# Self-attention's maxima from four column tiles, next to the value steps

## The chip, the core and the metric

The kernel runs on one core of a Trainium2 chip. Its engines work from queues of their own and wait for one another by semaphores: TensorE (PE; its weight loads are PEld), VectorE (DVE), ScalarE (ACT), GpSimd (POOL), and SyncE (SP), which here only issues transfers. The metric is the device time of one execution in microseconds. TensorE's results go to eight banks of on-chip memory, each 128 partitions by 512 floats.

## The reference

A decoder layer on x of 4 batches x 1024 tokens x 256 features, in float32. With 16 heads of 16 features:

```
qkv = layernorm(x) @ w_qkv                       # self-attention in chunks of 128 tokens
scores = q_chunk @ [k_previous_chunk, k_chunk].T / 4
scores masked where key > query, and where the previous chunk does not exist
x = x + softmax(scores) @ [v_previous, v_chunk] @ w_out
x = x + cross_attention(layernorm(x), ctx 77 keys, key mask)
x = x + ffn(layernorm(x))                        # 8-bit fake-quantised, inner width 704
```

So each query of self-attention sees the 128 keys of the chunk before its own and the keys of its own chunk up to itself.

## The kernel before, in words

Attention is cut into 16 jobs: self-attention (s) and cross-attention (x) of each batch, each in two halves a and b of eight heads, in the order S0a S0b S1a S1b S2a X0a S2b X0b S3a X1a S3b X1b X2a X2b X3a X3b. Each job has two groups, 0 and 1, of four heads. A group passes three kinds of TensorE steps. (Below, S1b-0 is group 0 of job S1b.)

A **maximum step** (lines 656 to 672) takes one chunk c of 128 queries. For each of the four heads one matmul forms scores of 128 queries against 256 keys (queries stationary, keys moving; the operands are bfloat16 parts whose products add up to float32 accuracy, 96 rows), two heads to a bank. One more matmul a bank adds the causal mask to the own-chunk columns of both heads. VectorE then reduces 4 x 256 columns to four negated maxima a query (line 1179). After the eighth chunk, "rows" splits the maxima into three bfloat16 parts with four short VectorE operations, "turnm" transposes them on TensorE (line 687), ScalarE copies them out (962) and issues a transfer (964) that puts them as three more rows below the queries. A **score step** (699) then multiplies with keys stationary, 99 rows: its result is already less the maximum, ScalarE takes the exponential (974), GpSimd clears what the causal mask hides (1451). A **value step** (737) multiplies with the values, 17 columns wide, on four column tiles: tile_position (0, 32i) puts each head on a quarter of the array's columns, and the four run at once. Cross-attention has its own three forms (677/679, 706/709, 748).

Results rotate over six banks. A maximum or score step needs two neighbouring ones, so three of them fit; a projection (qk 630, v 640, out 759) takes one. A step waits until the reader of its banks is through.

The order of all steps is written once, for all engines, by attention_order(). The table PLACE gives spans of each kind of work as shares of a period (LENGTH: 24.5 for a group of self-attention, 9.6 for cross); steps are spread evenly over their span and sorted by time. During the period of a group the maxima of the *next* group are placed ("max s0s" and so on). BEHIND says how many steps later a follower comes: turnm three after rows, a value step two score steps behind. Every engine goes through this list in order; one that waits holds up all that is behind it.

## Time and profile before

| | us |
|---|---|
| median of 3 runs | 851.69 (844.95 to 858.25) |
| profiled execution, span from first to last instruction | 849.0 |
| PE busy | 684.6 (81%) |
| DVE busy | 545.8 (64%) |
| ACT busy | 415.1 (49%) |
| POOL busy | 188.8 (22%) |
| self-attention maxima on DVE (line 1179), 128 reductions | 145.1 |
| mean granted TensorE clock | 0.911 |

Profile times count from the first instruction. The profiled execution's own time is its span of 849.0, 2.7 below the median. The granted clock of a stretch is 1.00 where TensorE had its full 2.4 GHz and 0.50 where it had 1.2 GHz. In a timeline row, the time is the start of the first of "xN" instructions and the length reaches to the end of the last; consecutive matmuls overlap, so the cost of a step is read from its start to the start of the next.

### The profile page before, as it was taken

The page shows a single profiled execution, that of the slowest core. Times are in us where ns is not written, and L with a number is a line of the kernel's source. Part 1 is how long each engine was busy: PE and PEld are TensorE (multiplying, and loading weights), DVE is VectorE, ACT ScalarE, POOL GpSimd, SP SyncE. Part 2 cuts the span into 40 slices and gives each one's busy share as a digit, 9 for nine tenths or more (in the row PEclk, how much of TensorE's full clock was granted, in tenths as well). Part 3 has the DMA queues.
Part 4 walks back from the last instruction along what each step waited for, and adds up shares of the span by engine and source line. Part 5 has one row for each costly group of instructions (what it writes and reads, how often), then busy time and mean ns, then how long its engine had stood idle before and what let it go on. Part 6 is the DMA issues. An engine that isn't in the chain of part 4 may idle for free.

```text
span 849.0 us, 14814 instructions
## 1 busy us (share of the span) xinstructions
PE 684.6 (81%) x5391; PEld 414.9 (49%) x5396; DVE 545.8 (64%) x975; ACT 415.1 (49%) x610; POOL 188.8 (22%) x231
## 2 busy tenths in 40 slices
PE   2579999989996998999979989897886784488565
PEld 1346565655653564556644644464543442233254
DVE  6277658866864456677636874556745651679996
ACT  2324665536463444555334446433343352399775
POOL 5002131312231120310113123002002000044436
PEclk9988999999997997999988989997998786699989
DMA  7534243502622153243222432331237112000013
GB/s 215 125 106 143 54 128 81 149 3 90 165 77 61 21 170 105 46 141 78 86 50 96 109 96 69 97 95 42 70 85 211 23 42 53 0 1 2 0 65 135
DMA packets 59557, 71.83 MB, mean 85 GB/s; under 512 B 25003, under 2 KB 36447, under 8 KB 59487
## 3 DMA queue, kind: packets, MB, share of 16 engines
q1 hardware_dynamic: 53391, 68.01, 29.2%
q10 hardware_dynamic: 6096, 2.88, 1.3%
q8 instruction: 44, 0.72, 0.4%
q14 instruction: 26, 0.21, 0.1%
HBM read 17.74 MB, written 4.72 MB: 26 GB/s over the span
## 4 chain that ended last, share of the span: by engine, by line
PE 49%; DVE 22%; issue 8%; ACT 7%; SPq 6%; DMA 6%; ACTq 1%; POOL 1%; POOLq 0%; DVEq 0%
PE banks L630 8%; PE banks L759 7%; PE banks L667 5%; PE banks L737 5%; DVE mneg L1179 4%; PE banks L699 4%; PE banks L640 3%; PE banks L748 3%; SPq L523 3%; PE banks L670 3%; DVE xn L1143 2%; SPq L517 2%; PE banks L706 2%; PE banks L709 2%; DVE tops L1358 2%
## 5 line engine op out<-in xcount | busy, mean ns | idle before, releaser
L1179 DVE TENSOR_REDUCE mneg<-banks 128x4 f32<-128x1024 f32 (+1 forms) x128 | 145.1, 1151 | 68.0 <-PE banks L670 67.5
L974 ACT ACTIVATE big<-banks 128x1024 f32<-128x1024 f32 (+1 forms) x128 | 123.0, 974 | 105.4 <-PE banks L699 101.7
L1451 POOL TENSOR_SCALAR_AFFINE_SELECT big<-big 128x512 f32<-128x512 f32 x128 | 83.1, 650 | 391.6 <-ACT big L974 390.9
L978 ACT ACTIVATE big<-banks 77x1024 f32<-77x1024 f32 x64 | 65.3, 1020 | 86.3 <-PE banks L709 81.8
L667 PE MATMUL banks<-big 96*128 96x256 bf16 (+1 forms) x512 | 94.5, 280 | 13.4 <-DMA big<-parts 9.8
L630 PE MATMUL banks<-xnT,weights 128*128 128x512 f32 x192 | 92.9, 617 | 3.9 <-ACT big L978 3.9
L699 PE MATMUL banks<-big 99*128 99x256 bf16 (+1 forms) x512 | 79.3, 280 | 13.3 <-DMA big<-m3t 5.7
L1183 DVE TENSOR_REDUCE mneg<-banks 128x8 f32<-128x616 f32 x64 | 50.3, 793 | 57.7 <-PE banks L679 57.6
L737 PE MATMUL banks<-big 128*17 128x256 f32 (+1 forms) x1152 | 79.0, 366 | 1.0 <-POOL big L1451 0.6
L670 PE MATMUL banks<-causal,identb 128*128 128x256 bf16 x256 | 72.9, 288 | 0.0
L667 PEld LDWEIGHTS banks<-big 96*128 96x128 bf16 x512 | 47.9, 103 | 45.9 <-issue 26.6
L699 PEld LDWEIGHTS banks<-big 99*128 99x128 bf16 x512 | 45.0, 101 | 48.3 <-issue 32.5
L803 PE MATMUL banks<-oe,weights 128*128 128x512 bf16 x187 | 46.8, 394 | 11.0 <-DVE big L1352 4.4
L630 PEld LDWEIGHTS banks<-xnT,weights 128*128 128x128 f32 x192 | 35.7, 197 | 38.1 <-issue 31.4
L677 PE MATMUL banks<-big 96*128 96x77 bf16 x512 | 43.1, 214 | 13.2 <-DMA big<-kparts 9.6
L706 PE MATMUL banks<-big 99*77 99x256 bf16 x256 | 51.1, 282 | 3.1 <-DVE big L1169 1.1
L677 PEld LDWEIGHTS banks<-big 96*128 96x128 bf16 x512 | 35.3, 108 | 32.9 <-issue 19.8
L709 PE MATMUL banks<-maskt,identb 77*77 77x512 bf16 x128 | 50.4, 394 | 0.0
L987 ACT COPY oe<-banks 128x512 f32<-128x512 f32 x64 | 37.2, 585 | 26.8 <-DMA oTx<-oe 10.9
L1224 DVE TENSOR_TENSOR xs<-banks,xs 128x512 f32<-128x512 f32 x32 | 22.1, 689 | 37.6 <-PE banks L759 37.6
L618 PE MATMUL banks<-ident,xn 128*128 128x128 f32 x128 | 23.7, 319 | 23.9 <-DVE xn L1143 23.5
L748 PE MATMUL banks<-big 77*17 77x256 f32 x512 | 42.7, 426 | 0.0
(155 smaller groups left out, 1163.8 us busy)
## 6 DMA issues: line engine op xcount, KB each, us to landing
big<-parts SPq DMA_DIRECT2D x282, 128.0 KB, 2.5
oc<-sums SPq DMA_DIRECT2D x16, 512.0 KB, 4.6
oTs<-oe SPq DMA_DIRECT2D x64, 64.0 KB, 2.3
out_dram<-oTs SPq DMA_DIRECT2D x16, 256.0 KB, 2.1
xs<-in_x_dram SPq DMA_DIRECT2D x3, 1024.0 KB, 5.8
big<-oe SPq DMA_DIRECT2D x32, 64.0 KB, 2.3
oTx<-oe SPq DMA_DIRECT2D x32, 64.0 KB, 2.3
big<-kparts SPq DMA_DIRECT2D x96, 9.6 KB, 1.8
```

The costliest lines, as they stand in the source:

```text
L630: t = e.matmul(bank(p), w[:, i, :], xnT[T][:, i, blk * 512:blk * 512 + 512], start=(i == 0), stop=(i == 1))
L667: e.matmul(bank(p, j)[:, i * 256 + lo * 128:i * 256 + 256], Q[0:96, hh, c * 128:c * 128 + 128], K[0:96, hh, (c - 1 + lo) * 128:(c + 1) * 1 ...
L670: t = e.matmul(bank(p, j).rearrange("p (s n) -> p s n", s=2)[:, :, 128:256], identb[:, :], causal[:, :].rearrange("p (a n) -> p a n", a=1) ...
L677: e.matmul(bank(p, j)[:, i * KX:i * KX + KX], Q[0:96, i, (c + j) * 128:(c + j) * 128 + 128], xks[r][0:96, i, :], start=(i == 0), stop=Fals ...
L699: t = e.matmul(bank(p, i // 2)[:, (i % 2) * 256:(i % 2) * 256 + n], ks[r][0:99, i, j * 128:j * 128 + 128], qs[r][0:99, i, j * 128:j * 128 ...
L706: e.matmul(bank(p, z)[0:KX, i * 256:i * 256 + 256], xks[r][0:99, 2 * z + i, :], qs[r][0:99, 2 * z + i, j * 256:j * 256 + 256], start=(i == ...
L709: t = e.matmul(bank(p, z)[0:KX, :].rearrange("p (i n) -> p i n", i=2), identb[0:KX, 0:KX], keep.to_broadcast([KX, 2, 256]), start=False, s ...
L737: t = e.matmul(acc[:, col // 512][32 * i:32 * i + 17, col % 512:col % 512 + z - a], va[f][:, j, 4 * g + i, :], P[:, i, a:z], start=new, st ...
L748: t = e.matmul(acc[:, j // 2][32 * i:32 * i + 17, (j % 2) * 256:(j % 2) * 256 + 256], xv[r][0:KX, i, 0:17], pt[u][0:KX, i * 256:i * 256 + ...
L974: e.activation(pt[u].rearrange("p (i n) -> p i n", i=4)[:, :, 0:n], pair(p).rearrange("p j (s n) -> p (j s) n", s=2)[:, :, 0:n], ACT.Exp, ...
L1179: e.tensor_reduce(M.rearrange("p (h c) -> p h c", h=4)[:, :, c], pair(p).rearrange("p j (s n) -> p (j s) n", s=2)[:, :, lo * 128:256], AX. ...
L1451: e.affine_select(out=P[:, :, 0:128], in_=P[:, :, 0:128], compare_op=ALU.is_ge, fill=0.0, base=0, pattern=[[0, 4], [1, 128]], channel_mult ...
```

## The change

**Queries in another order.** The qk projection of the queries reads its tokens permuted: for each half of 512 tokens, Q now holds a (which 32 of a chunk, 0 to 3), then the chunk t (0 to 3), then the 32 tokens. 128 neighbouring columns of Q are thus 32 queries of each of four chunks.

**Maximum step.** Step c = 4G + a takes these 128 queries. For each head there are four matmuls of 32 queries, one on each column tile, each over the keys of the chunk before (128) and the first 32a + 32 keys of its own: 160, 192, 224 or 256 columns. Chunk 0 has none before it, so there a matmul over key 0 repeated 128 times and one over the own keys stand in. The mask is added to the last 32 columns alone, by four matmuls of 2 x 32 columns a bank. A step has 24 matmuls (28 in the first half) where it had 6. The reduction reads 4 x (160 + 32a) elements a partition.

**Score step.** It gathers its queries from the new order; step 3 needs two matmuls of 128 a head instead of one of 256.

**Order.** beside() moves each maximum step of self-attention to the time of the nearest value step, directly behind it; rows stays where it was unless a step comes later.

```diff
@@ -123,6 +123,12 @@
     return [(span[0] + (span[1] - span[0]) * i / len(steps), step) for i, step in enumerate(steps)]
 
 
+def beside(timed, at):
+
+    near = [min(at, key=lambda v: abs(v - t)) for t, _ in timed]
+    return [(v + 0.0005, step) for v, (_, step) in zip(near, timed)]
+
+
 def stats_steps(kind, b):
     return [("stats", kind, b, c) for c in range(NC)] + [("root", kind, b, 0, NC)]
 
@@ -192,7 +198,8 @@
         job, units = JOBS[n], UNITS[JOBS[n][0]]
         kind, length = job[0], LENGTH[job[0]]
         nxt = JOBS[n + 1] if n + 1 < len(JOBS) else None
-        put([(-0.001, ("force", "rows"))] + over(PLACE["tail " + kind], tail))
+        ends = over(PLACE["tail " + kind], tail)
+        put([(-0.001, ("force", "rows"))] + ends)
         scores = over(PLACE["score " + kind], [("score", job, g, j) for j in range(units)])
         for j in range(units):
             put([scores[j]])
@@ -200,7 +207,12 @@
                 put([(scores[j][0] + 0.002, ("val", job, g, j - BEHIND["val"], False))])
         tail = [("val", job, g, j, j == units - 1) for j in range(units - BEHIND["val"], units)]
         if p + 1 < 2 * len(JOBS):
-            put(over(PLACE[f"max {kind}{g}{nxt[0] if g else kind}"], max_steps(p + 1)))
+            tops = over(PLACE[f"max {kind}{g}{nxt[0] if g else kind}"], max_steps(p + 1))
+            if JOBS[(p + 1) // 2][0] == "s":
+                values = [t for t, _ in ends] + [scores[j][0] + 0.002 for j in range(BEHIND["val"], units)]
+                tops = beside(tops[:-1], values) + tops[-1:]
+                tops[-1] = (max(tops[-1][0], tops[-2][0]), tops[-1][1])
+            put(tops)
         last = JOBS[n - 1] if n else ("s", 0, 0)
         if g == 0:
             if nxt:
@@ -627,8 +639,10 @@
                     e.wait_ge(a_xnT, 2 * n_of["turned", kind, b, 4 * blk])
                     w = wq_of(job, z)
                     for i in range(2):
-                        t = e.matmul(bank(p), w[:, i, :], xnT[T][:, i, blk * 512:blk * 512 + 512],
-                                     start=(i == 0), stop=(i == 1))
+                        tokens = xnT[T][:, i, blk * 512:blk * 512 + 512]
+                        if kind == "s" and z == 0:
+                            tokens = tokens.rearrange("p (t a b) -> p a t b", t=4, a=4)
+                        t = e.matmul(bank(p), w[:, i, :], tokens, start=(i == 0), stop=(i == 1))
                     t.then_inc(t_qk, 1)
                 elif k == "v":
                     _, job, c0 = s
@@ -660,16 +674,28 @@
                         if n_of[s] == 1:
                             e.wait_ge(p_set, 4)
                             e.wait_ge(d_set, 1)
-                        lo = 1 if c == 0 else 0
+                        G, a = divmod(c, 4)
+                        own = 32 * a + 32
                         for j in range(2):
                             for i in range(2):
                                 hh = 2 * j + i
-                                e.matmul(bank(p, j)[:, i * 256 + lo * 128:i * 256 + 256], Q[0:96, hh, c * 128:c * 128 + 128],
-                                         K[0:96, hh, (c - 1 + lo) * 128:(c + 1) * 128], start=(i == 0), stop=False,
-                                         skip_group_check=True)
-                            t = e.matmul(bank(p, j).rearrange("p (s n) -> p s n", s=2)[:, :, 128:256], identb[:, :],
-                                         causal[:, :].rearrange("p (a n) -> p a n", a=1).to_broadcast([128, 2, 128]),
-                                         start=False, stop=True, skip_group_check=True)
+                                for u in range(4):
+                                    q = Q[0:96, hh, c * 128 + 32 * u:c * 128 + 32 * u + 32]
+                                    to = bank(p, j)[32 * u:32 * u + 32, i * 256:i * 256 + 128 + own]
+                                    k0 = (4 * G + u) * 128
+                                    if k0:
+                                        e.matmul(to, q, K[0:96, hh, k0 - 128:k0 + own], start=(i == 0), stop=False,
+                                                 tile_position=(0, 32 * u), skip_group_check=True)
+                                    else:
+                                        e.matmul(to[:, 0:128], q, K[0:96, hh, 0:1].to_broadcast([96, 128]), start=(i == 0),
+                                                 stop=False, tile_position=(0, 0), skip_group_check=True)
+                                        e.matmul(to[:, 128:128 + own], q, K[0:96, hh, 0:own], start=False, stop=False,
+                                                 tile_position=(0, 0), skip_group_check=True)
+                            for u in range(4):
+                                late = causal[:, 32 * u:32 * u + 32].rearrange("p (s n) -> p s n", s=1)
+                                t = e.matmul(bank(p, j)[32 * u:32 * u + 32, :].rearrange("p (s n) -> p s n", s=2)[
+                                    :, :, 96 + own:128 + own], identb[:, 32 * u:32 * u + 32], late.to_broadcast([128, 2, 32]),
+                                    start=False, stop=True, tile_position=(0, 32 * u), skip_group_check=True)
                     else:
                         e.wait_ge(d_mask, 2)
                         for j in range(2):
@@ -694,11 +720,20 @@
                         if AT[job] < 2:
                             e.wait_ge(p_ones, r + 1)
                     if job[0] == "s":
-                        n = 256 if j < 7 else 128
                         for i in range(4):
-                            t = e.matmul(bank(p, i // 2)[:, (i % 2) * 256:(i % 2) * 256 + n],
-                                         ks[r][0:99, i, j * 128:j * 128 + 128], qs[r][0:99, i, j * 128:j * 128 + n],
-                                         start=(i % 2 == 0), stop=True, skip_group_check=True)
+                            to = bank(p, i // 2)[:, (i % 2) * 256:(i % 2) * 256 + 256]
+                            k = ks[r][0:99, i, j * 128:j * 128 + 128]
+                            q = qs[r][0:99, i, :].rearrange("p (g a u b) -> p g u a b", g=2, a=4, u=4)
+                            G, u = divmod(j, 4)
+                            if u < 3:
+                                t = e.matmul(to, k, q[:, G, u:u + 2, :, :], start=(i % 2 == 0), stop=True,
+                                             skip_group_check=True)
+                            else:
+                                t = e.matmul(to[:, 0:128], k, q[:, G, 3, :, :], start=(i % 2 == 0), stop=True,
+                                             skip_group_check=True)
+                                if G == 0:
+                                    t = e.matmul(to[:, 128:256], k, q[:, 1, 0, :, :], start=False, stop=True,
+                                                 skip_group_check=True)
                     else:
                         keep = maskt[0:KX, j * 256:j * 256 + 256].rearrange("p (a n) -> p a n", a=1)
                         for z in range(2):
@@ -1175,10 +1210,9 @@
                     M = mneg[:, rows_n[job, g] % 2, :]
                     e.wait_ge(t_max, n_of[s])
                     if job[0] == "s":
-                        lo = 1 if c == 0 else 0
                         e.tensor_reduce(M.rearrange("p (h c) -> p h c", h=4)[:, :, c],
-                                        pair(p).rearrange("p j (s n) -> p (j s) n", s=2)[:, :, lo * 128:256], AX.X, ALU.max,
-                                        negate=True).then_inc(d_max, 1)
+                                        pair(p).rearrange("p j (s n) -> p (j s) n", s=2)[:, :, 0:160 + 32 * (c % 4)],
+                                        AX.X, ALU.max, negate=True).then_inc(d_max, 1)
                     else:
                         e.tensor_reduce(M.rearrange("p (h c) -> p c h", h=4)[:, c:c + 2, :],
                                         pair(p)[:, :, 0:4 * KX].rearrange("p j (s n) -> p j s n", s=4), AX.X, ALU.max,
```

On TensorE, the end of S0a-0, from its turnm (before L687, now L713) to the first score step of S0a-1 (L699, now L729; with 128 columns it is the group's last). Before (L667 and L670 are maximum steps, L737 value steps, L618 transposes of normalised x):

```order
L687 MATMUL banks<-identb,m 96x128
L699 MATMUL banks<-big 128x256 x4
L737 MATMUL banks<-big 17x256 x4
L667 MATMUL banks<-big 128x256 x2
L670 MATMUL banks<-causal,identb 128x2x128
L618 MATMUL banks<-ident,xn 128x128 x8
L699 MATMUL banks<-big 128x128 x4
L737 MATMUL banks<-big 17x256 x4
```

Rows that only repeat the maximum steps are left out here: two whole ones stand before the L618 row, two more after the last row, then the first score step of S0a-1. Now (L772 value, L732 the last score step, L630 the transposes):

```order
L713 MATMUL banks<-identb,m 96x128
L772 MATMUL banks<-big 17x256 x4
L732 MATMUL banks<-big 128x128 x4
L772 MATMUL banks<-big 17x256 x4
L729 MATMUL banks<-big 128x256 x4
L630 MATMUL banks<-ident,xn 128x128 x8
L772 MATMUL banks<-big 17x256 x4
L690 MATMUL banks<-big 32x128
L692 MATMUL banks<-big 32x32
L687 MATMUL banks<-big 32x160 x3
```

Between turnm and the next group's first score step stood a score step more, the transposes and four maximum steps; now there are two value steps and the last score step. The next group's maxima begin after that first score step, seven in a row.

On VectorE, the same place (before L1179, now L1213, is the reduction of a maximum step; L1193 to L1199, now L1227 to L1233, are rows; L1143, now L1178, normalises x; L1152, now L1187, belongs to a projection). Before:

```order
L1199 TENSOR_TENSOR m<-mr,m 128x32
L1179 TENSOR_REDUCE mneg<-banks 128x4
L1143 TENSOR_SCALAR xn<-xs,mv,rstd 128x256 x4
L1179 TENSOR_REDUCE mneg<-banks 128x4 x7
L1152 TENSOR_TENSOR big<-banks,parts 128x512
```

Now:

```order
L1233 TENSOR_TENSOR m<-mr,m 128x32
L1178 TENSOR_SCALAR xn<-xs,mv,rstd 128x256 x4
L1213 TENSOR_REDUCE mneg<-banks 128x4 x8
L1187 TENSOR_TENSOR big<-banks,parts 128x512
```

The eight reductions were spread over score and value steps of two groups; now they all belong to the start of the second.

On VectorE again, X0a, whose two groups carry the maxima of X0a-1 (L1183, now L1217) and of S2b-0 (L1179, now L1213); L1154, now L1189, belongs to a projection. Before:

```order
L1183 TENSOR_REDUCE mneg<-banks 128x2x4 x2
L1179 TENSOR_REDUCE mneg<-banks 128x4
L1183 TENSOR_REDUCE mneg<-banks 128x2x4 x2
L1179 TENSOR_REDUCE mneg<-banks 128x4
L1193 CAST m<-mneg 128x32
...
L1179 TENSOR_REDUCE mneg<-banks 128x4
L1206 RECIPROCAL ls<-ls 128x64
L1179 TENSOR_REDUCE mneg<-banks 128x4 x4
L1154 SCALAR_TENSOR_TENSOR big<-banks,bias,parts 128x512
```

Now:

```order
L1217 TENSOR_REDUCE mneg<-banks 128x2x4 x4
L1227 CAST m<-mneg 128x32
...
L1240 RECIPROCAL ls<-ls 128x64
L1213 TENSOR_REDUCE mneg<-banks 128x4 x8
L1189 SCALAR_TENSOR_TENSOR big<-banks,bias,parts 128x512
```

On TensorE the eight maximum steps now stand between the two groups' score steps: six, a value step, two. The same happens in X0b and X1a. TensorE's runs of column-tiled work (value steps, and now maximum steps) number 168 in both orders.

## Rows read from the trace of the kernel before

**Rows 1.** The page: tenths of the time an engine is busy, 40 slices.
```profile
PE   2579999989996998999979989897886784488565
DVE  6277658866864456677636874556745651679996
PEclk9988999999997997999988989997998786699989
```
**Rows 2.** Busy time and granted clock, a stretch of S0b to S1b.
```profile
core 0: us, PE busy (x) PEld busy (x) DVE busy (x) ACT busy (x) POOL busy (x), PEclk, DMA share, GB/s
150.00:250.00 100.00, 92.44 (x825) 58.53 (x818) 71.04 (x125) 53.16 (x78) 25.47 (x37) 0.98 0.36 96
```
**Rows 3.** TensorE's timeline, value step 0 and maximum steps 4, 5 in S1b-0.
```profile
218.12 0.62 PE L737 MATMUL banks<-big 128*17 128x256 f32 x8
218.67 0.39 PE L667 MATMUL banks<-big 96*128 96x256 bf16 x2
...
219.44 0.38 PE L667 MATMUL banks<-big 96*128 96x256 bf16 x2
...
220.10 0.60 PE L699 MATMUL banks<-big 99*128 99x256 bf16 x4
```
**Rows 4.** TensorE's timeline, a first maximum step (151.12), and two value steps together.
```profile
151.12 0.28 PE L667 MATMUL banks<-big 96*128 96x128 bf16 x2
...
151.58 0.38 PE L699 MATMUL banks<-big 99*128 99x256 bf16 x2
...
152.78 0.84 PE L737 MATMUL banks<-big 128*17 128x256 f32 x16
153.55 0.61 PE L699 MATMUL banks<-big 99*128 99x256 bf16 x4
```
**Rows 5.** Groups by shape: the reductions, with busy us and mean ns.
```profile
L1179 DVE TENSOR_REDUCE mneg<-banks 128x4 f32<-128x1024 f32 x112 | 134.1, 1218 | 41.9 <-PE banks L670 41.5
L1179 DVE TENSOR_REDUCE mneg<-banks 128x4 f32<-128x512 f32 x16 | 11.0, 686 | 26.0 <-PE banks L670 26.0
```
**Rows 6.** TensorE's timeline: start of the very first maxima, and the projection after five.
```profile
42.44 0.37 PE L667 MATMUL banks<-big 96*128 96x128 bf16 x2 [8.79 <-DMA big<-parts]
...
48.37 0.86 PE L630 MATMUL banks<-xnT,weights 128*128 128x512 f32 x1
```
**Rows 7.** SP's timeline: first of its issues for X0a.
```profile
245.16 9.66 SPq L523 DMA_DIRECT2D big<-parts  x12
```
**Rows 8.** TensorE's timeline: the first maximum step of X0a, in S2a.
```profile
267.30 0.40 PE L677 MATMUL banks<-big 96*128 96x77 bf16 x4 [4.72 <-DMA big<-kparts]
```
**Rows 9.** TensorE's timeline in X0a: turnm, and the first score step of S2b-0.
```profile
324.79 0.26 PE L687 MATMUL banks<-identb,m 128*96 128x128 bf16 x1
...
329.47 0.37 PE L699 MATMUL banks<-big 99*128 99x256 bf16 x1 [2.43 <-DMA big<-m3t]
```
**Rows 10.** Windows: score step 5 to the work behind the last maximum; S0a, S0b, S1a, S1b.
```profile
79.12:93.94 14.82, 13.05 (x137) 8.51 (x134) 12.61 (x20) 7.39 (x12) 3.85 (x6) 1.00 0.02 3
124.55:135.92 11.37, 10.93 (x124) 7.00 (x120) 9.28 (x13) 5.78 (x10) 3.17 (x5) 1.00 0.22 53
164.99:185.23 20.24, 16.44 (x145) 10.99 (x142) 14.91 (x22) 7.38 (x12) 3.85 (x6) 0.92 0.14 33
221.19:236.47 15.28, 13.25 (x137) 8.46 (x134) 12.59 (x21) 7.39 (x12) 3.94 (x6) 1.00 0.38 85
```
**Rows 11.** TensorE's timeline in S1a-1: the output projection of batch 0.
```profile
179.13 3.39 PE L759 MATMUL banks<-weights,oTs 128*128 128x256 f32 x8 [1.99 <-DVE oTs L1216]
```
**Rows 12.** Windows: the wait of rows 9, what follows it, and a feed-forward stretch.
```profile
326.40:329.40 3.00, 0.64 (x10) 0.38 (x6) 2.93 (x8) 1.02 (x1) 0.00 (x0) 0.90 0.36 109
329.40:339.00 9.60, 9.53 (x55) 4.91 (x56) 5.32 (x10) 3.98 (x5) 1.27 (x2) 0.50 0.41 133
816.00:824.00 8.00, 5.91 (x48) 4.40 (x48) 8.00 (x9) 6.70 (x7) 5.17 (x5) 1.00 0.36 127
```
**Rows 13.** Window: the densest 24 matmuls in a row.
```profile
148.10:149.14 1.04, 1.03 (x24) 0.83 (x25) 0.28 (x1) 1.01 (x2) 0.64 (x1) 1.00 0.38 120
```

## The prediction

> **What bounds the kernel now.** I read the page's slices first. TensorE stands at nines from the third slice to about the 28th, VectorE mostly at six to eight: in self-attention the kernel runs at TensorE's pace [rows 1]. A window says the same: in 100 us TensorE is busy for 92.44, VectorE for 71.04 [rows 2]. Then I read the timeline step by step, each from its start to the start of the next. A maximum step (four matmuls of 256 columns, two masks of 256) takes 219.44 to 220.10, 0.66 us, back to back with its neighbours [rows 3]. That is 0.11 for 256 columns, or 0.43 ns a column. A value step takes 218.12 to 218.67, 0.55 [rows 3], but two together, the second of half the columns, take 152.78 to 153.55, 0.77 [rows 4]: part of a lone step is the change into and out of column tiling, which a neighbour shares. So what TensorE saves comes off the time only where it runs back to back. Last I looked for places where it stands, and for who holds it.
>
> **The change, part by part**
>
> *The step on TensorE.* Four tiles run at once in a value step. If the new matmuls do too, a round of four costs the columns of one: 160, 192, 224 or 256 at 0.43 ns, 0.07 to 0.11. Four rounds and two short mask rounds (64 columns, 0.03 each) make 0.33, 0.39, 0.44 and 0.50 for a = 0 to 3. Eight steps cost 3.3, against 0.46 (151.12 to 151.58) for the first [rows 4] and seven of 0.66: 5.1. That saves 1.8 a group, 28 in sixteen groups, gross. No row shows bfloat16 rounds of this length. The bounds are this, and a round as long as one of 256 columns now, six times 0.11: 0.66, no saving. I take the short one, because the value step is the same arrangement; the other end is a rival.
>
> *The reduction on VectorE.* 1024 elements take 1.218, 512 take 0.686 [rows 5], about 1.04 ns an element. So 640, 768, 896 and 1024 take 0.82, 0.95, 1.09 and 1.22: 8.2 for eight, where it was 9.2. VectorE's 145.1 falls to about 130. That counts where TensorE waits for VectorE. The mean, 1.02, is over twice TensorE's new 0.42, and this matters next.
>
> *Order.* Three pairs of banks fit. A run of more than three maximum steps therefore goes at VectorE's pace of 1.02. What the new order saves in changes of tiling is nothing: 168 column-tiled runs before and after. What it costs has to be added place by place.
>
> 1. S0a-0. Five steps take 42.44 to 48.37, 5.93, at half clock [rows 6]. Twice the new prices for five steps are 4.0, and three steps behind them also get cheaper: 2.4 gained.
> 2. Maxima that are needed in group 1 of S0a, S0b, S1a, S1b, S2b, S3b stand in ones and twos next to value steps of group 0; TensorE has no long wait there. 1.8 less about 0.35 of waits for a bank: 1.4 each, 8.6. In the last two, three steps are at half clock and gain about 0.7 more each. S0a has five in a row, 0.8 lost. Together 9.2 gained.
> 3. S2a and S3a: nothing. SP issues transfers for the cross job without a pause from 245.16 [rows 7], and TensorE then stands 4.72 for the last of them [rows 8]. That chain begins with a projection ahead of these maxima, so a faster TensorE only stands longer.
> 4. The handover from group 0 to group 1 of S0a, S0b, S1a, S1b. From turnm to the score step that needs its rows, the path (transpose, copy on ScalarE, transfer, landing) takes 324.79 to 329.47, 4.7, where TensorE had little left to do and stood 2.43 [rows 9]. At the four handovers this path was covered by four maximum steps, which are now moved behind the score step. What is left between is a value step, the short last score step (0.33) and another value step, 1.5. I take 4.4 for the path; 2.9 of idle time opens. Then seven maxima stand in a row behind one value step, an eighth behind the next. By the eight reductions in sequence, with a bank pair free when the third-last is read, the step behind them starts 8.5 after the group's first score step. From score step 5: 0.53, value 0.56, score 0.53, transposes with their wait 1.5, turnm 0.1, path 4.4, then transposes 0.9 and 8.5: 17.0 for S0a and S1b, which took 14.82 and 15.28 [rows 10]. S0b has no transposes: 14.5 against 11.37. S1a has an output projection more (1.7): 18.7 against 20.24; it gains, because that projection stood for VectorE's scaling, which was queued behind maxima and comes before them now [rows 11]. Sum: 5.5 lost.
> 5. The clock. A wait of 2.43 was followed by 9.6 us at 0.50 [rows 12]; the shorter one of 1.99 also led to a projection of 3.39 instead of 1.7 [rows 11]. Three of the four handovers get such a wait anew. Half clock costs nothing in a run that goes at VectorE's pace, so only some 3 us of TensorE's own work at half clock count: 1.5 each, 4.5 lost.
> 6. X0a, X0b, X1a. Eight maxima of the next self-attention job stood among the cross steps, 5.1. In one run they hold TensorE for about 6: 1.0 lost in each, 3.0. The 2.43 of rows 9 stays.
> 7. Score step 3 has two matmuls of 128 columns for one of 256: the same columns, nothing. The permuted reads take as many columns as before, nothing. GpSimd, SP and their transfers keep number and size.
>
> Sum: -2.4 - 9.2 + 5.5 + 4.5 + 3.0 = +1.4 on the span of 849.0, so 850.4. The profiled span is 2.7 below the median of the runs; on the median's scale this is **853**.
>
> **A rule to weigh.** The densest stretch is 24 matmuls, each with its weight load, in 1.04 us, 43 ns each [rows 13], and columns account for that. A new step asks for 24 to 28 in 0.42, some 16 ns each, for longer than any stretch shows. The Trainium skill (TensorE: Matmul & The Clock Gate, in "Wait — 56ns, not 53.3ns?") says that matmuls never start less than about 25 ns apart, and about 62 where the sequencer's software decodes them. Estimated from that page, a step would be 26 x 25 = 0.65, or 1.6; the sum would be about 865 by the first. No run here shows either.
>
> **The rivals**
>
> *TensorE is not fed fast enough (20%).* If 43 ns for each matmul is what can be kept up [rows 13], a step of 26 costs 1.1 instead of 0.42. Of 128 steps, 56 stand in the long runs, where VectorE's 1.02 hides nearly all of it, and 16 are in S2a and S3a, where the SP chain hides it. The other 56 lose 0.7 each, 39, and the 56 lose 0.1 each, 5. Waits and long float32 projections, during which instructions can gather, give some of it back: I take a fifth. 853 + 35 = **888**, slower. It decides from 26 ns a matmul upwards, where the step passes 0.66. For it speaks that nothing in the trace is as dense; against it, that the four of a value round take about the time of one.
>
> *The step stays at 0.66 (12%).* Rounds are no shorter than 0.11, because four separate weight loads don't hide behind 0.07 of columns, and the mask rounds have nothing to hide them. Places 1 and 2 lose their 11.6; the rest stays. **865**. The Trainium skill (TensorEngine Tiling, "Restrictions") has it that column tiling switches the fast weight load off; no row here shows what that costs.
>
> *The clock falls in the long runs (10%).* In a run of seven TensorE works 0.42 in 1.02. A feed-forward stretch that is busy 5.91 of 8 keeps 1.00 [rows 12]; nothing shows two fifths. If it falls, each of seven runs leaves 3.4 us of dense work at half clock, 1.7 each, 12: **865**.
>
> *The waits do not open (13%).* Maxima that end earlier let rows and turnm come earlier by about 2 us, VectorE has 15 less to do, and the small waits for it go. Then place 4 and the clock cost nothing, 10 better, and some 4 more come from VectorE: **839**.
>
> **How the numbers follow.** My forecast is that savings and new waits cancel: 853, 45% with its own range of 842 to 862. The range over all, **837 to 889**, leaves out a tenth at either end: below, the part of the last rival with larger savings; above, a feed at worse than 43 ns. A change of 2%, about what runs between 844.95 and 858.25 can tell, is 834.7 or 868.7. Faster by it: 8%, half of the last rival and a little of the forecast. Slower by it: 28%, nearly all of the first rival, and a third of the next two. The rest, 64%, is within.
>
> **What would show it.** TensorE's timeline: a whole maximum step in 0.33 to 0.50 from start to start, four matmuls of a round starting together; 0.65 or more is one of the first two rivals, and then whether it gets longer deep in a run tells them apart. Line 1213: 128 reductions, 130 us. TensorE idle 2 to 3 us before the first score step of group 1 in S0a, S0b, S1a, S1b, and granted clock 0.50 behind three of these. In the runs of seven, reductions back to back on VectorE. S2a still waits for SP near 267. I would be wrong if a step's price is off by over 0.1 in either direction, or if the path from turnm is much shorter than 4 us there.

## The result, and the profile after

The changed kernel takes 868.28 us (median of 4 runs, 863.44 to 874.48) where the kernel before takes 854.65 in the same series (4 runs, 844.95 to 858.25): 1.019 times as long, 95% interval 1.011 to 1.028. A second series gave 1.0235 (1.0185 to 1.0286). The prediction was 853 with a range of 837 to 889: inside the range, 15 above the value, and outside the 842 to 862 that the forecast gave itself. The profiled execution took 863.44, its span is 861.3; the span of before is 849.0, so 12.3 is what the traces have to explain. Executions of one kernel differ by nearly as much: when the changed kernel was profiled again, its span was 871.4. The account by places at the end therefore has both traces. The ratios compare fast runs alone, but kernels 3 and 5 below were profiled in slow ones, 863.12 and 881.48 against medians of 854.59 and 866.64, so what is read from these two traces is weaker.

The page of the changed kernel, the lines that answer to [rows 1]:

```profile
PE   2577988979787898799869988977889685488665
DVE  6276646765754346767536766447656560679886
PEclk9989999989989799999988989997997775799979
```

Many of TensorE's nines from the fourth slice on have become sevens and eights: it does less and stands more. Its waits over 60 to 260, grouped by what ended them (total us, times, longest):

```profile
PE banks L729 <- DMA big<-m3t: 14.9, 5, 4.1
PE banks L687 <- DVE mneg L1213: 3.5, 8, 0.6
PE banks L630 <- DVE xn L1178: 3.3, 7, 1.1
PE banks L713 <- DVE m L1233: 3.0, 4, 1.3
```

m3t is the tile with the three rows of maxima, on its way to the queries. In the kernel before no score step is shown to wait for it in that stretch. One of the five waits is no news, though: the very first score step of all, at 62.36, waits 4.06, and before it stood 3.29 in the same place, which the view calls "issue": nothing that the profile shows. The other four, 10.8 together, stand at the handovers from group 0 to group 1 and are new. The new step itself is as cheap as it was meant to be. TensorE's timeline, a value step and the start of each of five maximum steps in S0a-0:

```profile
67.56 0.63 PE L772 MATMUL banks<-big 128*17 128x256 f32 x8
68.00 0.22 PE L690 MATMUL banks<-big 96*32 96x128 bf16 x1
...
68.36 0.26 PE L687 MATMUL banks<-big 96*32 96x192 bf16 x3
...
68.80 0.28 PE L687 MATMUL banks<-big 96*32 96x224 bf16 x3
...
69.50 0.23 PE L690 MATMUL banks<-big 96*32 96x128 bf16 x1
...
70.37 0.32 PE L687 MATMUL banks<-big 96*32 96x160 bf16 x8 [0.17 <-DVE mneg L1213]
```

68.00 to 68.36 is 0.36 (28 matmuls), 68.36 to 68.80 is 0.44. At the Trainium skill's 25 ns from one matmul's start to the next (TensorE: Matmul & The Clock Gate, "Wait — 56ns, not 53.3ns?") 28 would take an estimated 0.70; on different column tiles this trace shows 13 ns, and the measurement decides. The steps are as cheap as this where nothing holds them; from the third on VectorE sets the pace: 0.70, 0.87, then 1.0. The reductions, where [rows 5] had 134.1 and 11.0:

```profile
L1213 DVE TENSOR_REDUCE mneg<-banks 128x4 f32<-128x640 f32 (+3 forms) x128 | 123.8, 1018 | 82.6 <-PE banks L696 82.3
```

The four handovers, from score step 5 of group 0 to the work behind the last maximum, as in [rows 10] (length; TensorE, weight loads, VectorE, ScalarE, GpSimd; clock, DMA share, GB/s):

```profile
77.56:96.53 18.97, 13.68 (x302) 8.94 (x294) 12.13 (x21) 6.98 (x12) 4.35 (x6) 0.91 0.02 4
125.44:141.55 16.11, 10.90 (x287) 7.73 (x280) 8.92 (x13) 5.04 (x10) 3.17 (x5) 0.89 0.20 47
170.28:191.84 21.56, 16.40 (x309) 10.53 (x301) 14.21 (x24) 6.85 (x12) 5.02 (x6) 0.84 0.14 35
227.57:249.86 22.29, 14.57 (x293) 9.12 (x293) 12.12 (x22) 6.79 (x11) 4.81 (x6) 0.85 0.28 63
```

Together 78.9 instead of 61.7: **17.2 more, in 9% of the span, and more than the 12.3 by which the whole span grew.** Here is S1b's on TensorE:

```profile
227.57 0.61 PE L729 MATMUL banks<-big 99*128 99x256 bf16 x4 [0.21 <-DVE mneg L1213]
...
230.36 0.41 PE L630 MATMUL banks<-ident,xn 128*128 128x128 f32 x2 [1.07 <-DVE xn L1178]
...
231.67 0.76 PE L630 MATMUL banks<-ident,xn 128*128 128x128 f32 x4 [0.27 <-DVE xn L1178]
232.84 0.23 PE L713 MATMUL banks<-identb,m 128*96 128x128 bf16 x1 [0.41 <-DVE m L1233]
...
233.89 0.63 PE L772 MATMUL banks<-big 128*17 128x256 f32 x8
238.66 1.01 PE L729 MATMUL banks<-big 99*128 99x256 bf16 x4 [4.15 <-DMA big<-m3t]
...
240.59 1.97 PE L630 MATMUL banks<-ident,xn 128*128 128x128 f32 x8
...
246.14 0.35 PE L687 MATMUL banks<-big 96*32 96x192 bf16 x8 [0.47 <-DVE mneg L1213]
...
247.27 0.38 PE L687 MATMUL banks<-big 96*32 96x224 bf16 x8 [0.56 <-DVE mneg L1213]
```

and on VectorE, GpSimd and ScalarE:

```profile
227.43 0.15 DVE L1170 TENSOR_SCALAR ve<-mv 128x8 f32<-128x8 f32 x1
227.50 1.22 DVE L1213 TENSOR_REDUCE mneg<-banks 128x4 f32<-128x1024 f32 x1
229.40 2.54 DVE L1178 TENSOR_SCALAR xn<-xs,mv,rstd 128x256 f32<-128x256 f32 x4 [0.68 <-POOL rstd L1475]
231.86 0.17 DVE L1227 CAST m<-mneg 128x32 bf16<-128x32 f32 x1
...
243.38 6.43 DVE L1213 TENSOR_REDUCE mneg<-banks 128x4 f32<-128x640 f32 x7 [9.39 <-PE banks L696]
```
```profile
227.72 1.64 POOL L1475 TENSOR_TENSOR rstd<-ve,halves 128x8 f32<-128x8 f32 x1 [2.26 <-ACT big L1009]
```
```profile
233.43 0.27 ACT L997 COPY m3t<-banks 96x128 bf16<-96x128 bf16 x1
233.73 0.76 ACTq L999 DMA_DIRECT2D big<-m3t  x1
```

Four things follow each other. Group 1's eighth maximum now stands behind a value step and ends just ahead of score step 5; its reduction, four scalings for the cross job and the casts are in VectorE's queue one behind the other, so turnm comes 5.3 after score step 5 (3.7 before). In S1a and S1b it isn't this reduction that the scalings wait for last. Here it ends at 228.72 and they start at 229.40, when GpSimd has rstd (the factor of the layer norm) ready. GpSimd needs ve for it, which VectorE used to make ahead of its last two reductions and now makes between them. Before:

```profile
218.73 0.11 DVE L1135 TENSOR_SCALAR ve<-mv 128x8 f32<-128x8 f32 x1
219.55 2.36 DVE L1179 TENSOR_REDUCE mneg<-banks 128x4 f32<-128x1024 f32 x2 [0.71 <-PE banks L670]
```

The scalings now start 1.8 after score step 5, where it was 0.6 before. From its transfer's issue at 233.73 the score step waits until 238.66, and TensorE stands for 4.15. What follows runs at half clock (score step 1.01 for 0.61, transposes 1.97 for 1.06). Then seven reductions stand back to back.

### The profile page after: what moved, and what is told of

The parts are those of the page before. It is cut to its first block, busy times and chain, and to the rows that moved or that the text cites. A ratio compares the mean times of both kernels' runs of the same rounds, so it can differ in the third digit from the quotient of the medians.

```text
span 861.3 us, 20067 instructions
## 1 busy us (share of the span) xinstructions
PE 671.6 (78%) x8015; PEld 413.4 (48%) x8020; DVE 527.4 (61%) x975; ACT 415.3 (48%) x610; POOL 189.1 (22%) x231
## 3 DMA queue, kind: packets, MB, share of 16 engines
q8 instruction: 65, 1.06, 0.5%
HBM read 17.74 MB, written 4.72 MB: 26 GB/s over the span
## 4 chain that ended last, share of the span: by engine, by line
PE 45%; DVE 21%; issue 9%; SPq 8%; DMA 8%; ACT 6%; POOL 1%; ACTq 1%; POOLq 0%; DVEq 0%
PE banks L645 8%; PE banks L794 7%; DVE mneg L1213 6%; PE banks L772 4%; SPq L529 3%; PE banks L783 3%; PE banks L654 3%; DMA big<-m3t 3%; PE banks L729 3%; SPq L535 3%; PE banks L741 2%; DVE xn L1178 2%; PE banks L744 2%; PE banks L703 2%; PE banks L630 2%
## 5 line engine op out<-in xcount | busy, mean ns | idle before, releaser
L1213 DVE TENSOR_REDUCE mneg<-banks 128x4 f32<-128x640 f32 (+3 forms) x128 | 123.8, 1018 | 82.6 <-PE banks L696 82.3
L1217 DVE TENSOR_REDUCE mneg<-banks 128x8 f32<-128x616 f32 x64 | 50.3, 794 | 65.2 <-PE banks L705 65.2
L772 PE MATMUL banks<-big 128*17 128x256 f32 (+1 forms) x1152 | 81.6, 372 | 1.1 <-POOL big L1485 0.6
L729 PE MATMUL banks<-big 99*128 99x256 bf16 x384 | 62.6, 291 | 24.9 <-DMA big<-m3t 20.4
L687 PE MATMUL banks<-big 96*32 96x160 bf16 (+3 forms) x1792 | 74.4, 268 | 8.0 <-DVE mneg L1213 6.2
L729 PEld LDWEIGHTS banks<-big 99*128 99x128 bf16 x384 | 33.6, 102 | 52.7 <-issue 37.5
L703 PE MATMUL banks<-big 96*128 96x77 bf16 x512 | 43.0, 214 | 18.6 <-DMA big<-kparts 14.6
L696 PE MATMUL banks<-causal,identb 128*32 128x64 bf16 x1024 | 55.3, 202 | 0.0
L703 PEld LDWEIGHTS banks<-big 96*128 96x128 bf16 x512 | 34.9, 107 | 38.0 <-issue 24.5
L687 PEld LDWEIGHTS banks<-big 96*32 96x32 bf16 x1792 | 42.1, 101 | 20.9 <-DVE mneg L1213 17.1
L630 PE MATMUL banks<-ident,xn 128*128 128x128 f32 x128 | 26.0, 338 | 26.7 <-DVE xn L1178 25.5
L690 PE MATMUL banks<-big 96*32 96x128 bf16 x256 | 37.6, 239 | 10.3 <-DMA big<-parts 8.7
```

The lines of the kernel that those rows point to most:

```text
L687: e.matmul(to, q, K[0:96, hh, k0 - 128:k0 + own], start=(i == 0), stop=False, tile_position=(0, 32 * u), skip_group_check=True)
L703: e.matmul(bank(p, j)[:, i * KX:i * KX + KX], Q[0:96, i, (c + j) * 128:(c + j) * 128 + 128], xks[r][0:96, i, :], start=(i == 0), stop=Fals ...
L729: t = e.matmul(to, k, q[:, G, u:u + 2, :, :], start=(i % 2 == 0), stop=True, skip_group_check=True)
L772: t = e.matmul(acc[:, col // 512][32 * i:32 * i + 17, col % 512:col % 512 + z - a], va[f][:, j, 4 * g + i, :], P[:, i, a:z], start=new, st ...
L1213: e.tensor_reduce(M.rearrange("p (h c) -> p h c", h=4)[:, :, c], pair(p).rearrange("p j (s n) -> p (j s) n", s=2)[:, :, 0:160 + 32 * (c % 4)],
```

## The experiments

All ratios are to the kernel before on the same chip; kernels 1 to 4, 5 to 8 and 9 to 12 ran on three different chips. "Four handovers" is the sum of the stretches above: 61.7 before, 78.9 after (78.7 when the changed kernel ran again). Two executions of the tiles alone differ by 2.0 in it (56.2 and 58.2), so a difference of 2 says little.

**1, 2. The two halves of the change apart.** Tiles without the order:

```
-            if JOBS[(p + 1) // 2][0] == "s":
-                values = [t for t, _ in ends] + [scores[j][0] + 0.002 for j in range(BEHIND["val"], units)]
-                tops = beside(tops[:-1], values) + tops[-1:]
-                tops[-1] = (max(tops[-1][0], tops[-2][0]), tops[-1][1])
             put(tops)
```

> The new tiled maximum steps in the order of the kernel before. Theory A (the loss lies in the order: the path from turnm to the next score step is no longer covered at four handovers, and runs of seven go at VectorE's pace): the handovers take again 11 to 20 us as in the kernel before, a maximum step stands at 0.4 to 0.6 (a lone one pays a change of tiling of about 0.2), and the time is below the kernel before's, 843 to 850. Theory B (the tiled steps themselves cost, by feeding or by what they do to the clock): the time stays near the changed kernel's 868, at least 862, with the old order as well. Theory C (both in equal parts): about 857.

Measured: 843.6, ratio 0.991 (0.987 to 0.996). In its trace:

```profile
78.92:93.03 14.11, 11.61 (x298) 8.11 (x294) 11.62 (x20) 7.44 (x12) 4.21 (x6) 1.00 0.02 6
123.08:133.65 10.57, 9.44 (x284) 6.52 (x280) 8.28 (x13) 5.83 (x10) 3.17 (x5) 1.00 0.23 58
162.01:179.61 17.60, 13.68 (x306) 9.58 (x302) 13.46 (x22) 7.43 (x12) 5.04 (x6) 1.00 0.21 46
218.03:231.93 13.90, 12.63 (x296) 9.19 (x294) 8.59 (x14) 6.87 (x11) 2.54 (x4) 0.88 0.27 61
```

Four handovers: 56.2, with the same tiled steps, and in three of them at full clock.

The order without the tiles (the diff's other hunks undone: the matmuls, the score step, the reduction and the order of the queries as before):

> The kernel before's maximum steps (0.66 us, reductions of 1.22) in the changed kernel's order. Theory A: all that the order costs and nothing that the tiles give: the four handovers +17 as in the changed kernel, and another 1.5 each because a run of eight reductions takes 9.2 instead of 8.2, and places 2 and 6 lose what the tiles saved there (about 6): 875 to 885, slower than both. Theory B: the order is harmless and takes changes of tiling away, so 852 to 860. Theory C: about 865.

Measured: 886.18, ratio 1.046 (1.042 to 1.051); four handovers 81.8. Theory A holds, and B and C fall: the tiles gain, the order alone loses 4.6%. The loss is even larger than expected (36 on the span): only 20.1 of it lies in the four handovers, and another 13 builds up between S2a and S3b. By the starts of the score steps, 12 of these come in S2b-0 (3.6), X0b (3.7) and S3b-0 (4.9); what causes them was not followed up.

**3, 4. Which part of the order.** The next job's maxima around group 1 where they were:

```
-            if JOBS[(p + 1) // 2][0] == "s":
+            if JOBS[(p + 1) // 2][0] == "s" and (g == 0 or kind == "x"):
```

> As the changed kernel, but the maxima of the next self-attention job that are issued around group 1 (S0a, S0b, S1a, S1b) stand where the kernel before had them; all others stay beside value steps. Theory A: the four waits of 1.7 to 4.2 us ahead of the first score step of group 1 go, and the runs of seven with them: 16 to 18 us back, 850 to 853. Rival D (the half-clock stretches are the cause and come with any gap): the waits go but only half of the time comes back, 858 to 862. Theory B: no more than 5 back, 863 or more.

Measured: 854.59, ratio 1.010 (1.006 to 1.014), between Theory A's range and Rival D's. Four handovers 63.8: 15.1 of the 17.2 are back there, and at all four the wait for m3t is gone (the one left from 60 to 260 is that of the very first score step). The ratio gives back less, 8 to 12 us; where the rest stays this trace can't tell. Of the 63.8, S1b keeps 17.56 where the tiles alone have 13.90: the transposes still wait 1.24 for the scaling, and run at half clock.

Beside value steps, but those of the group before as well (`values += [(t - start) / length for t in earlier]`, with `earlier` the value steps' times of the last group):

> As the changed kernel, but a maximum step may also stand beside a value step of the group before, the nearest in time: four or five of the next job's maxima then cover the path from turnm, in ones to threes, and the long runs are gone, also in the cross jobs. Theory A: the handovers are as short as in the kernel before and no step changes tiling alone: below the kernel before, 842 to 850. Rival E (what is gained at the handovers is lost by maxima that wait for VectorE or hold it against turnm's rows): 852 to 858. Theory B: 862 or more.

Measured: 860.17, ratio 1.0135 (1.0065 to 1.0205), four handovers 67.9. This misses Theory A, and lies 2 above Rival E's range. Maxima do cover the path, five at a time, but in S1a and S1b turnm to the score step takes 8.9 and 8.4: the waits for VectorE among these maxima are only 0.3 to 0.4 each, and much of TensorE's work there runs at half clock (granted 0.71 and 0.80 over the two handovers). In S1a the output projection waits 2.2 for VectorE again, as it did before. Beside a value step is no good place in itself.

**5, 6. The last two maxima of the group early.**

```
+                early = tops[6:8] if g == 0 else []
+                if early:
+                    values = [t for t in values if t < early[0][0]]
-                tops = beside(tops[:-1], values) + tops[-1:]
+                tops = beside(tops[:8 - len(early)], values) + early + tops[-1:]
```

> As the changed kernel, but the last two of a group's own eight maxima stand ahead of score step 4, where the kernel before had them, not behind value steps. Theory F (the transposes and turnm wait for the eighth maximum's reduction and what VectorE does behind it, so a step that is later by one place makes turnm later by 1.1 to 1.6): from score step 5 to turnm 3.7 to 4.2 us (S0b 1.7) instead of 4.7 to 5.3 (2.8); 1 back at each of four handovers and 1 in S2b and S3b, about 5 in all: 862 to 864. Rival G (turnm waits for the transposes' copy or for the clock, not for the maximum): both lengths as in the changed kernel, 867 to 870.

Measured: 866.64, ratio 1.020 (1.014 to 1.026): no gain that can be measured. Half of Theory F holds: from score step 5 to turnm it takes 3.3, 1.7, 3.8, 3.8 instead of 4.7, 2.8, 5.3, 5.3. Which half can't be told: the edit moves the last two reductions, and in VectorE's queue ve too comes 1.0 to 1.2 earlier, ahead of both, so the scalings don't wait for rstd either. But of the 5.5 gained there, 3.6 were lost again from turnm to the score step. TensorE and ScalarE in S1b:

```profile
231.13 0.23 PE L716 MATMUL banks<-identb,m 128*96 128x128 bf16 x1
...
237.94 1.01 PE L732 MATMUL banks<-big 99*128 99x256 bf16 x4 [5.02 <-DMA big<-m3t]
```
```profile
231.72 1.04 ACT L1012 ACTIVATE big<-banks 128x1024 f32<-128x1024 f32 x1
232.63 0.27 ACT L1000 COPY m3t<-banks 96x128 bf16<-96x128 bf16 x1
```

turnm's copy now stands behind an exponential on ScalarE (231.13 to 232.63, 1.5, the same in S1a; in the changed kernel 0.6), and the score step starts 10.6 after score step 5, where it was 11.1. Four handovers: 77.1.

The same, and the next job's maxima as before (`== "s" and g == 0`):

> Only a group's own maxima one to six stand beside value steps; its last two, and all that are issued for the next job, stand as in the kernel before. Theory A with F: the four handovers are as in the kernel with the old order (17.8, 14.2, 23.9, 15.7 from score step 5 to score step 2 of group 1, within 0.5), the first part keeps its gain of 2, and the cross jobs keep theirs: 1.0% below the kernel before, 838 to 844 on its scale of 849. Rival H (what a step beside a value step saves in changes of tiling is lost again in waits for a bank pair on VectorE, since three or four then come in a row): no faster than the kernel with the old order, 844 to 850.

Measured: 843.08, ratio 0.995 (0.990 to 1.000), four handovers 55.8 (12.9, 13.0, 17.3, 12.6). The path is covered. Against the tiles alone S0a, S1a and S1b are 1.2, 0.3 and 1.3 shorter and S0b 2.4 longer, where TensorE stands 1.45 for nothing that the profile shows. The median lies in the expected 838 to 844, but the kernel before took 850.96 here; on its scale of 849 the ratio gives 845, which is Rival H's. Whether this beats the tiles alone the intervals don't tell.

**7. The wait filled.**

```
+                        again = {0: 6, 1: 8, 2: 4, 3: 11}.get(AT[job], 0) if (g, j) == (0, 7) else 0
-                        for i in range(4):
+                        for i in list(range(4)) * (1 + again):
```

> As the changed kernel, but the short last score step of group 0 of S0a, S0b, S1a, S1b is repeated in place 6, 8, 4 and 11 times more (0.33 us each: 2.0, 2.6, 1.3, 3.6), so TensorE works through most of the wait for turnm's rows; the output doesn't change. Theory J (the wait itself lowers the granted clock and what follows at half clock costs some 4.5 us in all): no stretch at 0.50 behind these four places, 3 to 5 us less, 863 to 865. Rival K (half clock there costs nothing, since the seven maxima go at VectorE's pace): the stretches are gone, the time is the same within 1, 867 to 869. Rival L (the clock falls in the runs of seven themselves): the stretches at 0.50 stay, and the time.

Measured: 870.36, ratio 1.025 (1.020 to 1.029). Its first two handovers:

```profile
80.13:97.73 17.60, 13.48 (x326) 9.20 (x318) 12.00 (x21) 6.76 (x12) 4.37 (x6) 1.00 0.02 5
126.63:143.16 16.53, 11.68 (x320) 8.05 (x312) 8.90 (x13) 5.16 (x10) 3.18 (x5) 1.00 0.22 50
```

The granted clock is 1.00 where it was 0.91 and 0.89, in runs of seven too, so Rival L falls. In S1a and S1b it still is 0.84; in S1b it fell behind the waits of the transposes, ahead of the filling. Four handovers 76.4: 2.5 less. It divides: from group 1's first score step on the four are 4.4 shorter (37.5 for 41.8), about the 4.5 that the prediction had for the clock; from turnm to that step they are 2.0 longer (21.0 for 19.0), mostly because in S1a and S1b the filling outlasted the wait: TensorE no longer waits for m3t there. The time as a whole shows nothing of it: 870.36 is above what both J and K expected, and its own uncertainty is larger than what would part them.

**8. A short reduction** (`[:, :, 0:32]` for `[:, :, 0:160 + 32 * (c % 4)]`):

> As the changed kernel, but each of the 128 reductions reads only the first 32 columns of a tile (128 elements, about 0.3 us, for 1.02); the maxima are therefore not the true ones. Theory A (a run of seven goes at VectorE's pace): the runs of seven go at 0.4 to 0.5 a step, from score step 0 to score step 1 of group 1 takes 5 us less at each of four handovers (9.2 becomes 4), 20 in all, the eighth reduction ends 0.9 earlier in each group, some 5 more, and the waits ahead of group 1's first score step stay at 2 to 4: 840 to 846. Rival M (long runs are slow because TensorE isn't fed with 26 matmuls each 0.42): no more than 5 at the handovers, 858 to 866.

Measured: 847.91, ratio 0.999 (0.995 to 1.003), some 17 to 21 under the changed kernel, and 2 above Theory A's range. A run in S1b without VectorE's pace, and VectorE beside it:

```profile
235.88 0.32 PE L687 MATMUL banks<-big 96*32 96x160 bf16 x8
...
236.22 0.35 PE L687 MATMUL banks<-big 96*32 96x192 bf16 x8
...
236.62 0.38 PE L687 MATMUL banks<-big 96*32 96x224 bf16 x8
```
```profile
236.12 1.04 DVE L1213 TENSOR_REDUCE mneg<-banks 128x4 f32<-128x128 f32 x3 [0.23 <-PE banks L696]
```

0.34 and 0.40 a step where the run stood at 1.0 to 1.13: VectorE's pace was the limit, and Rival M falls as the main cause. But the handovers give back only 9.0 (69.9), not 20: I had not taken the half clock off (the first steps of this run take 0.64 to 0.80), and TensorE now shows something new (below). The waits for m3t stay (15.6 over the same stretch, 14.9 in the changed kernel, the very first 4.1 in both): the path from turnm costs by itself. And turnm still comes 3.8, 1.7, 4.2 and 5.0 after score step 5: with reductions of 0.3 the scalings wait 0.3, 0.3 and 1.1 for GpSimd's rstd.

**9 to 12. On one chip.** The changed kernel again; the cross jobs' share of the order undone (`and (g == 0 or kind == "s")`); the tiles alone again; and tiles with only S0a's own maxima moved (`if p == 0:` in kernel 5).

> The changed kernel once more, on the chip of the next three, so that their ratios can be set beside its own: 1.019 times the kernel before, within 0.006. If the filled wait (1.0246) and the last two maxima early (1.0203) truly gave back 2 to 5 us, it comes out above 1.022; if they gave nothing, at 1.015 to 1.022.

> As the changed kernel, but the eight maxima of the next self-attention job that stand among the cross steps of X0a, X0b, X1a stand there as in the kernel before. By the prediction's place 6 (1.0 lost in each where they hold TensorE in a run): 3 less than the changed kernel, 0.4%. By what the two traces show there (0.3 in all, the run has no wait of its own): the same within 1; and if single steps among cross steps pay for two changes of tiling (0.2 each, 24 steps), up to 4 more.

> The new tiled maximum steps in the kernel before's order, once more beside the changed kernel: 0.991 times the kernel before (0.987 to 0.996), and 2.5 to 3% under the changed kernel, so the order's share of the change's loss is 20 to 24 us.

> The new tiled maximum steps; only maxima one to six of S0a's group 1 stand beside value steps (with the last two ahead of score step 4), all others stand in the kernel before's order. S0a-0 gains 2 by the traces (its maxima ahead of score step 5: -2.1 where the old order had +0.3), and nothing else changes: 2 under the kernel with tiles alone, 0.987 to 0.990 times the kernel before. If the first part's gain came from something else that the order moved there, it is the same as with tiles alone, 0.991 or more.

| kernel | us | ratio (95%) | four handovers |
|---|---|---|---|
| before | 851.58 | 1 | 61.7 |
| changed | 868.76 | 1.0235 (1.0185 to 1.0286) | 78.7 |
| cross jobs as before | 866.97 | 1.0197 (1.0151 to 1.0244) | 78.4 |
| tiles alone | 843.79 | 0.9925 (0.9884 to 0.9965) | 58.2 |
| tiles, first part moved | 841.38 | 0.9888 (0.9853 to 0.9922) | 54.0 |

The order costs 868.76 - 843.79 = 25.0 and the tiles give 7.8. Neither is a fixed price: with the old steps the order costs 4.6%, 39 (kernel 2), so in the new order the tiles give 19 to 23, by the difference of the ratios. Of the 25.0, 78.7 - 58.2 = 20.5 lie in the four handovers. The cross jobs are worth 1.8 or nothing. The changed kernel came out above 1.022, so by its expectation kernels 5 and 7 may have given a little back; but its two series lie 0.4% apart, more than would be given back by either. The last kernel has the lowest median, 1.1% under the kernel before, as expected, but its interval overlaps that of the tiles alone, and between their two traces only 0.8 of the 8.2 in the spans has come in by the first score step of S0a-1, where the gain was looked for.

## Why the prediction was right, and where it was wrong

The place and the mechanism of the loss were right; the balance was not. The forecast was that savings and new waits cancel (+1.4), and they don't: the medians differ by 13.6, in the second series by 17.2. That the time still lies inside 837 to 889 is luck in part: the range reached above 862 for a slow feed, steps of 0.66 and a clock that falls in the long runs, and none of these came. By the prediction's places, on the profiled spans, read at the starts of score steps:

| place | predicted | measured | profiled again |
|---|---|---|---|
| 1. S0a-0, the first maxima | -2.4 | -1.7 | -1.5 |
| 2. a group's own maxima | -9.2 | -6.2 | -2.7 |
| 3. S2a and S3a | 0 | +1.3 | +0.3 |
| 4, 5. four handovers, with the clock | +10.0 | +17.2 | +17.0 |
| 6. cross jobs | +3.0 | +0.3 | +3.3 |
| not foreseen: waits of transposes in S2b, S3b | 0 | +3.7 | +3.8 |
| sum | +1.4 | +14.6 | +20.2 |

The span grew by 12.3: 3.1 came back behind the last score step of S3b, where no instruction changed, and 0.8 more was lost in the rest of S2b-1. In the second trace it grew by 22.4, with 0.6 lost behind S3b and 1.7 in the rest of S2b-1 and S3b-1. So the handovers and the transposes' waits are firm, and the smaller places are known to some 3. (In every later run the time is 2.1 to 2.4 above the span, so most of the 2.7 that the prediction added is this offset, and not a profiled execution that was faster than the median.)

- **The step's price: right.** Predicted 0.33, 0.39, 0.44, 0.50; measured 0.36, 0.40 to 0.44, 0.46, 0.51. The two rivals that doubted it fall with it: "TensorE is not fed fast enough" (20%) and "the step stays at 0.66" (12%). So does "the clock falls in the long runs" (10%), by kernel 7. "The waits do not open" (13%) is refuted by 10.8 of TensorE's idle time in four places.
- **VectorE's pace: right.** A reduction takes 1.018 on average for 1.02, all of them 123.8 for about 130 forecast (overlapping ones count once), and runs go at 1.0 to 1.13 with the reductions back to back.
- **The SP chain in S2a: right.** The first maximum of the cross job comes at 281.39 where [rows 8] had 267.30, behind transfers that begin at 258.62 [rows 7]:

```profile
281.39 0.42 PE L703 MATMUL banks<-big 96*128 96x77 bf16 x4 [6.19 <-DMA big<-kparts]
```

 Both moved by 13.5 to 14.1: TensorE's earlier saving there only made the wait longer, 6.19 for 4.72.
- **Place 4 is the step that failed, in size.** The waits themselves came as forecast in sum, 2.4, 3.1, 1.2 and 4.2 for 2.9 each; the work on either side was longer. Its path had 1.5 for "transposes with their wait" between score step 5 and turnm, read where the eighth maximum stands ahead of score step 4. In the new order it stands ahead of score step 5, and what VectorE does behind it is late: 4.7, 2.8, 5.3, 5.3 to turnm where the terms gave 3.1, 1.6, 3.1, 3.1. That is 7.1 of the difference. In S1a and S1b the scalings start 1.1 and 1.2 later than before against score step 5, and by the trace it is GpSimd's rstd that they wait for last, since ve too moved behind a reduction; the prediction had no term for that. The four scalings also take 2.5 for 2.1 there. The path from turnm took 4.0, 5.2, 3.9, 5.8 for 4.4 each, 1.4 more: 4.0 where the queues carry little (DMA share 0.05 over the wait in S0a), and 5.2 and 5.8 in S0b and S1b beside other transfers (0.41 and 0.42). The share alone doesn't decide it: in S0b the path took 3.6 in kernel 8 and 4.0 in kernel 2, at shares of 0.41 and 0.49. Why it was long in these two stays open.

```profile
83.30:86.30 3.00, 0.66 (x10) 0.13 (x9) 0.14 (x1) 1.07 (x2) 0.63 (x1) 1.00 0.05 11
129.80:133.40 3.60, 0.59 (x9) 0.10 (x8) 0.00 (x0) 1.88 (x3) 1.27 (x2) 1.00 0.41 106
233.90:238.70 4.80, 0.65 (x11) 0.19 (x10) 0.09 (x1) 1.07 (x2) 0.63 (x1) 0.85 0.42 114
238.66:244.00 5.34, 5.33 (x81) 3.64 (x85) 0.62 (x1) 2.10 (x3) 0.63 (x1) 0.50 0.01 3
```

 The rows are the waits of S0a, S0b and S1b, and what follows the last. From group 1's first score step on it took 3.5 more than the terms gave, with half clock inside it. 7.1 + 1.4 + 3.5 = 12.0, less the 4.5 that place 5 had set aside for the clock, is 7.5; the table has 7.2.
- **How the order's cost divides.** The changed kernel against the tiles alone, adding up the gaps between TensorE's matmuls from score step 5 to score step 2 of group 1: 95.0 against 71.7. Idle ahead of turnm 6.4 against 2.4, from there to the first score step 10.8 against 4.0, behind it 6.6 against 2.4, and the same instructions busy for 71.2 against 62.9, since they run at half clock in part. All four are of the order's making. Filling the second (kernel 7) took the last to 76.0, of which 29 repeats of 0.33 are 9.6: at least 4.8 less, since some repeats ran at half clock.
- **Place 5:** half clock came at all four handovers, not three (the windows' 0.91, 0.89, 0.84, 0.85). In S1a, which the prediction had 1.5 faster since its output projection no longer waits, that projection took 3.1 at half clock, and the handover came out 1.3 longer.
- **Place 2: the saving was too large.** A step that is 0.3 to 0.4 cheaper on TensorE gave 6.2 over six groups in one trace and 2.7 in the other, not 9.2. In the first S0a gave nothing, S1a and S1b 0.3 and 0.2, and around the maximum steps of S1b-0 TensorE stands 0.2 to 0.3 each time, mostly for VectorE's last reduction. Even in the old order the tiles gave 7.8 of the 28 that TensorE's prices promise. **Place 6** stays open: 0.3 in one trace, 3.3 in the other, 4.0 of it in X0b alone, and 1.8, within the uncertainty, when it was undone.

## What to carry to other kernels

- Work that is moved away from a latency path is part of the price of the move. Before moving it, list for every path with a transfer what TensorE does between its start and its end; the four steps moved here had covered waits of 1.2 to 4.2, and the order cost three times what the tiles saved.
- A step that is made later by one place moves everything that hangs on its result, and small neighbours in another engine's queue that a third engine waits for (here ve, for rstd), so a path's length can't be read from the old order: redo it with the new place. Two changes that come together should be timed apart: here one is 0.8% faster and the other 4.6% slower.

## What the runs showed that was not expected

- Matmuls on four column tiles start much denser than any stretch before: 24 to 28 in 0.34 to 0.51, 13 to 21 ns each, with a weight load each. This is no limit of its own over one run of seven. But small stalls turn up beside them. In the trace of the short reduction, and among the waits of the tiles alone:

```profile
93.52 0.40 PE L687 MATMUL banks<-big 96*32 96x256 bf16 x6 [1.23 <-issue]
```
```profile
PE banks L768 <- issue: 2.2, 1, 2.2
```

 TensorE waited there for nothing that the profile shows. The kernel before has one of 3.3, ahead of the very first score step, where most later traces name m3t, and beyond it none over 0.4 from 60 to 260. Of the twelve traces with tiled steps nine have one to four more over 0.4, up to 2.2 each, and three have none, the changed kernel's own first trace among them; when it ran again it had two (1.1 and 0.5). So they explain none of its loss in that stretch. Whether instructions come too slowly there was not tested; if so, it is a small part of the first rival that did come.
- Half clock can come behind short waits in a row as well, but not each time: in S1b of kernel 7 TensorE stood 1.07, 0.21 and 0.26 between transposes, and the last four took 1.01 instead of 0.76 in all. In S1b of the changed kernel it stood 1.07, 0.20 and 0.27 in the same place, and they took 0.76. In S1a of the changed kernel the clock was at 0.50 already ahead of the wait for m3t.
